# One-hots of six or five edge chunks in one VectorE comparison instead of two ScalarE activations per chunk

## Time and profile before

| | us |
|---|---|
| median of 3 runs | 5813.71 (5810.03 to 5819.62) |
| the profiled execution, its own time | 5817.22 |
| its span in the trace | 5815.1 |
| relational pass, chunk loop, in the trace | about 4463 to 5113 |
| last pass, chunk loop, in the trace | about 5237 to 5790 |

### The profile page before, as it was taken

The page is one execution under the profiler, slowest core; times in us unless marked ns, Lnnn a source line. Parts: engine busy times, 40 slices in busy tenths (PEclk is TensorE's granted clock), DMA queues, the critical chain, the costliest instruction groups (busy, mean ns, idle before and its releaser), DMA issues. The chain is left out here.

```text
span 5815.1 us, 117211 instructions
## 1 busy us (share of the span) xinstructions
PE 4146.4 (71%) x23177; PEld 3355.2 (58%) x23178; DVE 3130.0 (54%) x8630; ACT 2635.5 (45%) x8246; POOL 3935.3 (68%) x4447
## 2 busy tenths in 40 slices
PE   3499995777786666776666845555678877748886
PEld 2277774666675555565555634444666666626675
DVE  4455554555445555455555554444432777765655
ACT  0155553444435555445555333333123666617775
POOL 0066665888867888778888668888566777607775
PEclk9699997999999999999999966666888888867777
DMA  6533336444433333423333246556334434554444
GB/s 115 116 123 124 123 123 101 112 113 112 110 45 107 101 101 101 78 70 101 101 101 101 30 147 174 174 173 171 52 112 124 105 104 104 91 54 107 107 107 100
DMA packets 591389, 627.58 MB, mean 108 GB/s; under 512 B 318574, under 2 KB 485380, under 8 KB 591236
## 3 DMA queue, kind: packets, MB, share of 16 engines
q0 software_dynamic: 163968, 423.88, 28.5%
q1 hardware_dynamic: 368164, 190.45, 13.8%
q10 hardware_dynamic: 59104, 11.80, 1.2%
HBM read 481.69 MB, written 143.25 MB: 107 GB/s over the span
## 5 line engine op out<-in xcount | busy, mean ns | idle before, releaser
L883 POOL DMA_INDIRECT G<-h_dram,idx x1872 | 1850.1, 988 | 521.1 <-issue 423.8
L982 PE MATMUL ps_a<-hotm,msg 128*128 128x128 f32 x5616 | 905.6, 284 | 562.4 <-POOL hotm L874 520.8
L982 PEld LDWEIGHTS ps_a<-hotm,msg 128*128 128x128 f32 x5616 | 810.3, 192 | 798.9 <-POOL hotm L874 559.6
L975 PE MATMUL ps_e<-nnw,attT 128*128 128x256 f32 x2808 | 853.7, 387 | 95.7 <-DVE prodm L1043 32.4
L1050 DVE TENSOR_TENSOR arena<-ps_a,arena 128x256 f32 x1404 | 588.5, 419 | 360.9 <-PE ps_a L982 306.1
L656 POOL DMA_INDIRECT rec_dram<-rec,pos x392 | 382.9, 977 | 521.3 <-ACT rec L532 454.6
L1019 ACT ACTIVATE msg<-prodm 128x256 f32<-128x256 f32 x936 | 388.5, 415 | 634.9 <-DVE prodm L1043 526.1
L847 ACT ACTIVATE dist<-iota,meta 128x128 f32<-128x128 f32 x1716 | 659.3, 393 | 35.3 <-ACTq L228 28.1
L1202 PE MATMUL ps_a<-arena,msg 128*128 128x128 f32 x1872 | 387.5, 382 | 336.3 <-POOL arena L874 299.9
L883 POOL DMA_INDIRECT G<-feat_dram,idx x420 | 409.7, 975 | 288.1 <-POOLq L188 160.4
L1043 DVE TENSOR_TENSOR prodm<-G,ps_e 128x256 f32<-128x256 f32 x936 | 390.9, 418 | 371.6 <-DMA G<-h_dram,idx 319.5
(11 more groups left out here) (285 smaller groups left out, 7996.3 us busy)
## 6 DMA issues: line engine op xcount, KB each, us to landing
gate<-rec_dram SPq DMA_DIRECT2D x156, 384.0 KB, 3.3
G<-h_dram,idx POOLq DMA_INDIRECT x1872
rel_dram<-stage SPq DMA_DIRECT2D x25, 1040.0 KB
attT<-attT_dram SPq DMA_DIRECT2D x104, 144.0 KB, 2.6
rec_dram<-empty SPq DMA_DIRECT2D x1, 11242.0 KB, 71.6
at<-edge_attr SPq DMA_DIRECT2D x98, 112.0 KB
rec_dram<-empty SPq DMA_DIRECT2D x75, 146.0 KB, 5.6
h_dram<-hs SPq DMA_DIRECT2D x75, 128.0 KB, 1.7
```

Of the source, the lines that this page charges most:

```text
L883: pool.indirect_dma_start(G[:, n % width, :], None, table, bass.IndirectOffsetOnAxis(ap=idx[:, which, n:n + 1], axis=0)).then_inc(sem(f"sw ...
L975: t.matmul(ps_e[s % BANKS][:], attT[:, s // HU, s % HU, :], nnw[:], start=True, stop=True).then_inc(sem("ew"), 1)
L982: last = t.matmul(ps_a[s % BANKS][:, h, :], msg[:, s % RING, h * P:(h + 1) * P], hot[:, s, :], start=True, stop=True)
```

## The change

ScalarE no longer makes one-hots in these two passes. VectorE makes them with one `tensor_tensor` comparison for `HR` = 6 chunks (relational pass) or `Q3` = 5 chunks (last pass): the iota of 128 columns, repeated for each chunk, against each chunk's column of places, repeated along 128 columns. It stands at step n for chunks n to n + 5 (n to n + 4); in the relational pass behind the add and the message of that step, in the last pass ahead of them. TensorE waits for it once per six or five chunks. The buffer `dist` goes away in both passes; the ring `hot` keeps its 36 and 20 slots. The first layers' one-hots are unchanged.

```diff
+UR, GR, HR = 36, 12, 6
...
+        def one_hots(v, rows, to):
+
+            width = rows.shape[1]
+            v.tensor_tensor(to, iota[:, 0:P].unsqueeze(1).to_broadcast([P, width, P]),
+                            rows.unsqueeze(2).to_broadcast([P, width, P]), ALU.is_equal).then_inc(sem("hots"), 1)
...
@@ relational pass, TensorE @@
-                                    pe.wait_ge(sem("hot"), upto(n))
+                                    if s % HR == 0:
+                                        pe.wait_ge(sem("hots"), i * (UR // HR) + s // HR + 1)
...
@@ relational pass, ScalarE @@
-                            for c0, c1, c2, c5, c12 in walk(nc.scalar, TURNSR, 0, 1, 2, 5, 12, width=UR):
-                                if c0:
-                                    one_hot_distance(act, c0, meta[:, ds(c0[0]), 0], dist)
-                                if c1:
-                                    n, i, s = c1
-                                    act.wait_ge(sem("agg"), upto(n - UR))
-                                    one_hot_row(act, c1, dist, hot[:, s, :])
+                            for c2, c5, c12 in walk(nc.scalar, TURNSR, 2, 5, 12, width=UR):
...
@@ relational pass, VectorE, behind the add (c28) and the message (c26) @@
+                                if c0 and c0[2] % HR == 0:
+                                    n, i, s = c0
+                                    dve.wait_ge(sem("agg"), upto(n + HR - 1 - UR))
+                                    one_hots(v, meta[:, ds(n, HR), 0], hot[:, s:s + HR, :])
...
@@ last pass, TensorE @@
-                                    pe.wait_ge(sem("hot"), upto(n))
+                                    if s % Q3 == 0:
+                                        pe.wait_ge(sem("hots"), i * BATCHES + s // Q3 + 1)
...
@@ last pass, VectorE, ahead of the add (c12), the scores (c2_) and the message (c7) @@
+                                if c0 and c0[2] % Q3 == 0:
+                                    n, i, s = c0
+
+                                    dve.wait_ge(sem("agg"), upto(n + Q3 - 1 - U3))
+                                    one_hots(v, meta2[:, ds(n, Q3), 0], hot[:, s:s + Q3, :])
```

More of the change, by code:

```diff
@@ L64 @@
 G2, GROUPS2 = 3, 2
-UR, GR = 36, 12
+UR, GR, HR = 36, 12, 6
 RW = D + NH
@@ L1428, in relational_attention @@
                     hotT = sb(pctx, "hotT", [P, RING, P])
-                    dist = sb(pctx, "dist", [P, 2, P])
                     of_rel = sb(pctx, "of_rel", [P, NC1, R8])
@@ L1497, in _ @@
                         def _(act):
-                            credit(act, "dist", "hot", "hotT_sb", "ga", "fell", "w")
-                            for c0, c1, c2, c5, c12 in walk(nc.scalar, TURNSR, 0, 1, 2, 5, 12, width=UR):
-                                if c0:
-                                    one_hot_distance(act, c0, meta[:, ds(c0[0]), 0], dist)
-                                if c1:
-                                    n, i, s = c1
-                                    act.wait_ge(sem("agg"), upto(n - UR))
-                                    one_hot_row(act, c1, dist, hot[:, s, :])
+                            credit(act, "hotT_sb", "ga", "fell", "w")
+                            for c2, c5, c12 in walk(nc.scalar, TURNSR, 2, 5, 12, width=UR):
                                 if c2:
@@ L1535, in _ @@
                             bucket = Buckets(nc, mybir.EngineType.DVE, bmap[0:1, 1, :], T - 1, 28, width=UR, part=GR)
-                            for c5, c6, c7, c8, c10, c11, c12, c26, c28 in walk(nc.vector, TURNSR, 5, 6, 7, 8, 10, 11, 12, 26, 28, width=UR):
+                            for c0, c5, c6, c7, c8, c10, c11, c12, c26, c28 in walk(nc.vector, TURNSR, 0, 5, 6, 7, 8, 10, 11, 12, 26, 28, width=UR):
                                 if c28:
@@ L1814, in _ @@
                         def _(act):
[L1815 to L1824, removed]
+                            credit(act, "hotT_sb", "bounded", "w")
+                            for c2, c5 in walk(nc.scalar, TURNS2, 2, 5, width=U3):
                                 if c2:
@@ L1845, in _ @@
                             bucket = Buckets(nc, mybir.EngineType.DVE, bmap[0:1, 2, :], T - 1, 12, width=U3, part=2 * Q3)
-                            for c2_, c7, c12 in walk(nc.vector, TURNS2, 2, 7, 12, width=U3):
+                            for c0, c2_, c7, c12 in walk(nc.vector, TURNS2, 0, 2, 7, 12, width=U3):
+                                if c0 and c0[2] % Q3 == 0:
+                                    n, i, s = c0
+                                    dve.wait_ge(sem("agg"), upto(n + Q3 - 1 - U3))
+                                    one_hots(v, meta2[:, ds(n, Q3), 0], hot[:, s:s + Q3, :])
                                 if c12:
```

## The result

The changed kernel takes 5838.12 us (median of 6 runs, 5831.57 to 5841.71), the kernel before 5812.93 us in 6 runs beside it: ratio 1.0041 [1.0028, 1.0054]. It is slower by 25 us. The forecast was 5838 in a range of 5810 to 5878. The place of each term is another matter: in the relational pass the size came out, its cause did not.

A forecast was written before the change was run, and what follows sets the result against it. No engine was taken to bound the whole; VectorE, TensorE and ScalarE's loop paces the relational pass, gathers the last. +12 and +12 us gave +24, 5841 on the profiled execution and 5838 on the median, range 5810 to 5878.

The forecast's parts named there:

- Last pass, +12: Last pass: gather-bound, so 84 comparisons delaying gathers on GpSimd cost 12 us with nothing to cover them.
- holds: Both passes: gathers on GpSimd delayed until a VectorE operation on two SBUF inputs ends; 16 us relational, 12 us last.
- Relational pass, +12: Relational pass: VectorE's turn sets the pace, 0.95 us longer than 47.95, over 13 turns.
- 6.5 us a turn "without any releaser": VectorE's relational loop: idle for register loads and the jump back, 5.0 us in one piece, kept in the forecast.
- 34.1 + 5.3 + 6.5 + 3.0: VectorE's relational turn: busy now, added comparisons, idle without releaser, waits for TensorE; 48.9 us.
- the gathers' 47.4 us: Relational turn of GpSimd's gathers with their delays, 45.0 + 36 x 0.032 + 16 / 13, below VectorE's 48.9.
- 3.0 us of waits: VectorE's waits for TensorE in a relational turn, the middle taken between bounds 0 and 6.0 us.
- rival 3: Relational loop quickens to the gathers, VectorE's waits for TensorE near 0: +5, last pass +17, 5831 us; chance 0.12.
- slot waits: GpSimd's waits for a free slot ahead of relational gathers: 13 us, of which rival 3 usefully saves 10.
- the stall: VectorE's standing at the relational loop's jump back, 5.0 us in one piece of the 6.5 us without releaser.
- 0.8 x (L - 0.14)^2 / 2.5: Both passes: mean delay of gathers per VectorE operation of length L falling anywhere; 16 and 12 us for the comparisons.
- The relief of ScalarE: Both passes: 369 and 331 us removed from ScalarE, worth nothing by itself.

The follow-up runs named there:

- unused_comparison: Kernel before, ScalarE's one-hots kept, plus the change's comparisons on VectorE into a buffer nothing reads: 6485.1 us against 6530.3, ratio 0.9927.
- unused_reduction: Kernel before plus an unread tensor_reduce (one SBUF input, same elements) as often as the change compares: 6488.1 us against 6530.3, ratio 0.9931.
- last_only: Kernel before with the change in the last pass alone: 6503.7 us against 6530.3, ratio 0.9963.
- twice_after: Changed kernel with each gather of the two passes issued twice, the second into unread slots: 6963.05 us, ratio to the kernel before 1.1966.
- longer_loop_body: Kernel before with twelve long-satisfied waits added in VectorE's relational loop: 6363.4 us against 6407.9, ratio 0.9939.
- shifted_loop_body: Kernel before with twelve tiny memsets ahead of VectorE's relational loop, the loop itself unchanged: 6359.4 us against 6407.9, ratio 0.9932.
- scalar_compare: Changed kernel with one tensor_scalar per chunk in place of each six- or five-chunk comparison: 6345.3 us against the kernel before's 6407.9, ratio 0.9904.
- short comparisons: Changed kernel with two chunks a comparison (relational) and one (last), in two sets: 6353.3 against the kernel before's 6407.9, 6481.9 against 6530.3 us.
- twice_short: Changed kernel with two- and one-chunk comparisons and each gather issued twice, the second into unread slots: 6954.05 us, ratio to the kernel before 1.1948.

## Why the prediction was right, and where it wasn't

**Last pass, +12: right in mechanism and size.** Measured +11.3 us from first to last gather, the mean gather 1.002 us ("near 1.00"), holds +11.2 us, idle time ahead of gathers unchanged. 29 gathers are held to a comparison's end, for 12.4 us; those held by messages lost 1.5 us less than before. VectorE had the room and TensorE's granted clock rose, from 0.77 to 0.82 as the mean. That the comparisons do it is shown by unused_comparison against unused_reduction. That it is their two SBUF inputs fits the add and the message beside each other, but it is not the whole condition, since a `tensor_scalar` holds too. The inference in the Trainium skill, page "SBUF — State Buffer", section "Who interferes with whom", that descriptor generation isn't stalled by a `tensor_tensor`, falls with the same pair: 1.038 against 0.961 us a gather in the last pass.

**Relational pass, +12: right in size, by the wrong step.** The forecast kept 6.5 us a turn "without any releaser", made VectorE's turn 48.9 us from 34.1 + 5.3 + 6.5 + 3.0, and let the gathers' 47.4 us hide under it. The first two terms were right: 39.16 us busy against 39.4. The third was taken as fixed and went to nothing. Without it and with the bound of 3.0 us of waits VectorE's turn is 42.4 us, the gathers' is longer, and the pass goes by them: 47.84 us a turn. This is rival 3's mechanism, given 0.12. It priced the pass at +5, and the actual sum is made of its terms at other sizes: holds +21.8 instead of +15, slot waits -11.0 instead of -10, and the tail +1.2. So the +12 of the record is an agreement of two numbers and not of two reasons; on the same sizes rival 3 would have forecast about +12 as well. What rival 3 lacked was the way in: it wanted the waits for TensorE near 0, and they were 7.1 us in the turn against 6.0, harmless because the stall had gone. The forecast's sum has a second slip: 34.1 + 6.5 + 6.0 is 46.6 us, not the 47.95 of the turn it compares with, so 1.3 us of small idle pieces fell out. With them its turn would have been 50.2 us and the pass +30.

**The size of the holds.** 0.8 x (L - 0.14)^2 / 2.5 gave 16 us for 78 comparisons. In the trace 43 gathers were held to the end of one and lost 21.0 us, 0.27 us a comparison against 0.205. The lock of the two engines is the likely reason, as the same hold returned turn after turn; that was seen, not varied by itself. In the last pass it was 0.148 us a comparison against 0.143. That agreement is partly luck: with 84 of the same comparisons last_only had 35.6 us of such holds and twice_after 2.0, so the meetings decide and the formula, which lets operations fall anywhere, doesn't size them.

**Why the stall went.** It was not part of what the change does: the shifted loop loses the same packets with its code unchanged. In the changed kernel VectorE's loop has grown, and its code may lie elsewhere too; by what rule a place is good or bad stays open. So does what the stall itself cost in the kernel before under the conditions of the main result: longer_loop_body and shifted_loop_body gained 0.6 to 0.7% only where the kernel before took 6,408 us. With 11.4 us of slot waits there, the gathers leave 11 us to gain at most. What the change would cost with the stall still in place, no run shows; by the forecast's turn of 48.9 us against the measured 47.84 it would be 13 x 1.06 = 14 us more, an estimate.

**The relief of ScalarE** shows no gain at 5,838 us, as forecast: 520 us less work, and both passes go by their gathers. No run separates it from the rest of the change, and scalar_compare gained 63 us beside a kernel before of 6,408 us with the stall still there, so under those conditions it may be worth something.

**Open.** Whether scalar_compare or short comparisons beat the kernel before in its ordinary 5,813 us was not measured; their holds (9.4 and 12.7; 9.9 and 9.5 us) make it likely that they would cost less than the change does, but twice_short shows that such holds can grow where gathers set the pace. A comparison with its iota in PSUM wasn't tried, though the add with its PSUM input makes it the next thing to try; both passes already hold eight PSUM tiles.

## What to carry to other kernels

Where GpSimd's indirect DMAs pace a loop, look at the length of each single `tensor_tensor` or `tensor_scalar` on SBUF operands and not at their sum alone: a hold lasts to the end of one operation. One comparison for six chunks is cheaper for VectorE (74 us against 106) and was dearer for the gathers (holds of 37 us against 9) than six `tensor_scalar`. How often the two meet is set by the rhythm of the loop, so read it from the trace. Before costing an edit, ask of every idle piece "without releaser" whether it belongs to the work or to the place of the code; it may vanish with any edit, and the pace then passes to the next engine. And when a total agrees with the forecast, check its parts: here two wrong numbers, a stall that left and holds that stayed uncovered, made one right sum.

## What the runs showed of the hardware that was not expected

- An indirect gather of 128 rows is held to the end of a VectorE operation on two SBUF inputs that covers its first 0.14 us or so, and then takes 0.83 us more: 1.74 us beside 0.95 us of comparison. A `tensor_scalar` of 0.30 us holds it as well (20 gathers in scalar_compare, up to 0.12 us each). A `tensor_reduce` of 0.876 us doesn't (0.4 us over 74 gathers), nor does an add with one input in PSUM (0.3 us over 93).
- Instruction packets in a hardware loop depend on where its code lies: about five a turn and 5 to 6 us of standing at each jump, or next to none, for the same loop behind twelve more instructions.
- The same kernel on the same chip took 6,530 us in one set and 5,822 us in another. In the profiles of the long sets TensorE's granted clock is 0.79 to 0.84 over the whole span, against 0.87 and 0.88 in the kernel before and the changed one. The cause is not known from these runs.
